# Turns of the attention cut by round instead of by forty units, VectorE's preparation in smaller steps, and rotated tiles turned in TensorE's transpose mode

## The reference

```python
B, S, _ = x.shape                                   # 4, 2048; H = 16 heads, D = 16, K = 4 nodes
node_probs = softmax(x @ Wr)                        # per token, head: 4 probabilities
expected_pos = cumsum(node_probs over tokens) - node_probs
pos = clip(expected_pos, 0.0, MAX_SEQ - 1)
cos, sin = table at floor(pos), linearly interpolated by frac(pos)
cos_w, sin_w = sum over nodes of node_probs * cos, node_probs * sin
q_r = q * cos_w + rotate_half(q) * sin_w            # k_r the same
node_w = einsum('bhik,bhjk->bhij', node_probs, node_probs)
scores = q_r k_r^T * SCALE + log(node_w + 1e-08)    # causal mask
out = softmax(scores) @ v, then @ Wo
```

## Time and profile before

| | |
|---|---|
| median of 3 runs | 2926.09 us (2920.56 to 2927.48) |
| the profiled execution's own time | 2932.58 us |
| its span, first to last instruction | 2930.5 us |
| mean granted TensorE clock over the span | 0.919 of full speed |
| attention, about | 430 to 2560 us of the span |

### The profile page before, as it was taken

How to read it: one execution, slowest core, us unless ns; L and a number is a source line. 1 busy time by engine, 2 the same in 40 slices (tenths; PEclk the granted TensorE clock), 3 DMA queues, 4 the chain that set the end, 5 groups by cost and what they waited for, 6 DMA issues and landing times. The chain is left out here.

```text
span 2930.5 us, 104065 instructions
## 1 busy us (share of the span) xinstructions
PE 2469.0 (84%) x45964; PEld 1911.6 (65%) x45964; DVE 1713.9 (58%) x3605; ACT 1674.0 (57%) x2102; POOL 990.7 (34%) x1423
## 2 busy tenths in 40 slices
PE   7278635587999999899999989999999999972786
PEld 4155412366688887778888777888778888741554
DVE  7733178888576567766566776656675111177331
ACT  6022133456677776667777767777766777560221
POOL 1078710243232224422222442322243222110787
PEclk9589966799999999999999999999999999985888
DMA  6455411121211112212111221111222111161555
GB/s 230 136 102 103 73 41 29 48 63 38 65 56 52 52 45 79 65 50 60 54 51 56 76 63 53 60 53 51 67 65 67 47 47 47 55 230 22 103 101 74
DMA packets 185106, 207.24 MB, mean 71 GB/s; under 512 B 35984, under 2 KB 151712, under 8 KB 184480
## 3 DMA queue, kind: packets, MB, share of 16 engines
q1 hardware_dynamic: 158880, 165.60, 18.6%
q0 software_dynamic: 24576, 34.10, 7.2%
q10 hardware_dynamic: 1152, 0.26, 0.0%
HBM read 131.68 MB, written 76.02 MB: 71 GB/s over the span
## 5 line engine op out<-in xcount | busy, mean ns | idle before, releaser
L1624 PEld LDWEIGHTS at_mix<-at_val,at_ew 128*64 128x64 f32 x34816 | 1227.6, 138 | 238.1 <-issue 35.4
L1208 ACT ACTIVATE at_ew<-at_ring 128x1024 f32<-128x1024 f32 (+1 forms) x1280 | 1125.3, 898 | 364.5 <-PE at_ring L1606 358.4
L1624 PE MATMUL at_mix<-at_val,at_ew 128*64 128x68 f32 x34816 | 1266.9, 224 | 41.1 <-DVE at_mixed L1470 28.1
L1606 PE MATMUL at_ring<-at_qT,at_kT 98*64 98x512 bf16 (+3 forms) x5120 | 699.7, 353 | 56.9 <-ACT at_ew L1208 36.0
L1129 POOL TENSOR_SCALAR_AFFINE_SELECT at_ew<-at_ew 128x256 f32<-128x256 f32 x512 | 294.4, 579 | 1077.8 <-ACT at_ew L1208 1076.9
L1470 DVE TENSOR_TENSOR at_mixed<-at_mix,at_prob 128x272 f32<-128x272 f32 x256 | 112.3, 439 | 440.0 <-PE at_mix L1624 438.6
L1606 PEld LDWEIGHTS at_ring<-at_qT,at_kT 98*64 98x64 bf16 x5120 | 228.7, 112 | 110.8 <-ACT at_ew L1208 48.2
L1151 POOL TENSOR_TENSOR at_val<-at_vo,at_val 128x256 f32<-128x256 f32 x384 | 266.7, 715 | 7.5
L315 POOL DMA_INDIRECT ffn_xn<-table,ffn_idx_all x128 | 123.8, 968 | 310.6 <-DMA ffn_idx_all<-ffn_idx_hi 272.2
L325 POOL DMA_INDIRECT out_dram<-ffn_xn,ffn_idx_all x128 | 210.3, 1643 | 52.6 <-issue 37.1
L1689 PE MATMUL at_side<-at_w_all,at_turned 128*64 128x512 f32 (+1 forms) x1024 | 203.5, 543 | 13.3 <-DVE at_bounded L1463 4.7
(11 more groups left out here) (224 smaller groups left out, 2769.9 us busy)
## 6 DMA issues: line engine op xcount, KB each, us to landing
table<-ffn_xn SPq DMA_DIRECT2D x32, 512.0 KB, 6.2
q_parts<-at_parts SPq DMA_DIRECT2D x64, 192.0 KB, 2.4
k_parts<-at_parts SPq DMA_DIRECT2D x64, 192.0 KB, 3.0
at_qT<-q_parts SPq DMA_DIRECT2D x128, 96.0 KB
at_kT<-k_parts SPq DMA_DIRECT2D x64, 192.0 KB
ffn_front<-in_L_attn_x_dram SPq DMA_DIRECT2D x16, 512.0 KB, 5.2
ffn_w_in<-in_L_ffn_w_dram SPq DMA_DIRECT2D x32, 256.0 KB, 3.8
at_xin<-out_dram SPq DMA_DIRECT2D x32, 256.0 KB, 5.8
```

What stands on the lines that cost most here:

```text
L1208: act.activation(ew[u % NE_BUF][:, a:b], ring[u % 2][:, a:b], ACT.Exp).then_inc(s["exp_ready"], 1)
L1606: lastm = pe.matmul(ring[u % 2][h:h + HALF, at:at + (CH - t) * P], kT[q][:, kc + j * P + h:kc + j * P + h + HALF], qT[q][:, qc + t * P:qc ...
L1624: m = pe.matmul(mix[block_of[u] % 2][h:h + HALF, t * K * VW:(t + 1) * K * VW], ew[u % NE_BUF][:, col + h:col + h + HALF], val[q][:, tile0 ...
```

## The change

1. Turns are cut by round. The first four stay at 24 units (SHORT, kind 0). Each second round gets 6 turns, of 37, 37, 38, 37, 37, 38 units (LONG, kind 1); each first round after the first gets 2 turns of 48 (WIDE, kind 2). There are 34 turns as before, and each turn has the same pairs new, fin and post.
2. A third table for WIDE on every engine, BURST = 28 there, and changed tables for the other two kinds.
3. VectorE's steps are cut: positions into positions, whole_positions and first_angles; angles into count_turns and angles; rotate into two halves and join_halves; in LONG and WIDE turns node_products and node_sums into four pieces each. No instruction is added or removed but that the pieces of 2048 elements become pieces of 1024 there.
4. turn_rotated on PE makes 8 full tiles in transpose mode instead of 16 matmuls of half a tile with the identity as moving operand.

```diff
-    SHORT, LONG = 24, 40
-    N_SHORT = 4
+    SHORT, LONG, WIDE = 0, 1, 2
+    SHORT_SIZE, N_SHORT = 24, 4
+    TURNS = {1: 6, 0: 2}
...
-    turns, at = [], 0
-    while at < U:
-        m = len(turns)
-        turns.append((at, SHORT if m < N_SHORT else LONG))
-        at += turns[-1][1]
+    rounds = [first_unit[v] for v in range(V) if v == 0 or visits[v][1] != visits[v - 1][1]] + [U]
+    turns = [(m * SHORT_SIZE, SHORT_SIZE, SHORT) for m in range(N_SHORT)]
+    assert rounds[1] == N_SHORT * SHORT_SIZE
+    for r in range(1, len(rounds) - 1):
+        size, count = rounds[r + 1] - rounds[r], TURNS[r % 2]
+        marks = [rounds[r] + size * n // count for n in range(count + 1)]
+        turns += [(a, b - a, LONG if r % 2 else WIDE) for a, b in zip(marks, marks[1:])]
...
-        return turns[m][0] + (18 if m < N_SHORT else 24) if m >= 0 else 0
+        return turns[m][0] + STORE_AT[turns[m][2]] if m >= 0 else 0
...
-        BURST = 26
+        BURST = (None, 26, 28)
...
-                    if at == (10 if short else 14) and new is not None:
+                    if at == (10, 14, 16)[kind] and new is not None:
                         add_up(new)
...
-                SHORT_AT = (3, 6, None, 8, 9, 12, 15, 18, 16, 23, 20)
-                LONG_AT = (4, 6, 10, 8, 16, 18, 20, 23, BURST + 2, BURST + 4, BURST + 3)
+                SHORT_AT = (3, 6, None, 8, 9, 12, 15, 19, 17, 23, 16)
+                LONG_AT = (4, 6, 10, 8, 16, 18, 20, 23, 28, 30, 25)
+                WIDE_AT = (3, 6, 10, 9, 19, 22, 25, 28, 30, 35, 27)
...
-                SHORT_AT = (0, 1, 6, 8, None, 10, 12, 13, 14, 18, 19, 20, 21, 23)
-                LONG_AT = (1, 2, 5, 8, 10, 14, 17, 20, 22, 30, 32, 25, 34, 33)
+                AT = {"weights": (1, 1, 1), "rotate": (2, 2, 10), "rotate_2": (2, 3, 13), "join": (3, 4, 14), "squares": (14, 20, 26),
+                      "bound": (20, 25, 31), "residual": (None, 10, 12), "shift": (6, 5, 6), "softmax": (8, 8, 9),
+                      "positions": (10, 14, 16), "whole": (10, 14, 17), "first_angles": (11, 15, 18), "count_turns": (12, 17, 20),
+                      "angles": (13, 18, 22), "statistics": (15, 22, 24), "normalise": (23, 36, 46)}
+                PRODUCTS_AT = ({18: 0, 21: 2}, {30: 0, 32: 1, 33: 2, 34: 3}, {34: 0, 37: 1, 40: 2, 43: 3})
+                SUMS_AT = ({19: 0, 22: 2}, {31: 0, 33: 1, 34: 2, 35: 3}, {36: 0, 39: 1, 42: 2, 45: 3})
...
                             for n in range(4):
                                 for g in range(G):
-                                    for h in range(0, P, HALF):
-                                        at = (g * 4 + n) * P + h
-                                        lastm = pe.matmul(side[h:h + HALF, n * GP + g * P:n * GP + (g + 1) * P],
-                                                          qkr[:, at:at + HALF], ident[:, :],
-                                                          start=(n % 2 == 0 and g == 0), stop=False, skip_group_check=True)
+                                    at = (g * 4 + n) * P
+                                    lastm = pe.matmul(side[:, n * GP + g * P:n * GP + (g + 1) * P], qkr[:, at:at + P], ident[:, :],
+                                                      is_transpose=True, start=(n % 2 == 0 and g == 0), stop=False, skip_group_check=True)
...
                 SHORT_AT = (1, 4, None, None, 9, 10, 13, 16, 19, 21)
-                LONG_AT = (1, 3, 7, 9, 13, 15, 17, 20, 24, BURST)
+                LONG_AT = (1, 3, 7, 9, 13, 15, 17, 20, 24, 26)
+                WIDE_AT = (1, 4, 8, 11, 15, 20, 23, 26, 30, 33)
```

More of the change, by code:

```diff
@@ L987, in schedule @@
             first_visit()
-            for m, (start, size) in enumerate(turns):
-                for at in range(min(size, U - start)):
-                    unit(start + at, at, size == SHORT, new_of(m), fin_of(m), posts.get(m))
+            for m, (start, size, kind) in enumerate(turns):
+                for at in range(size):
+                    unit(start + at, at, kind, new_of(m), fin_of(m), posts.get(m))
             last_projections()
@@ L1059, in first_visit, with unit @@
                     load_heads(1)
-                def unit(u, at, short, new, fin, post):
+                def unit(u, at, kind, new, fin, post):
                     if u + 2 in first_unit and u + 2 < U:
@@ L1546, in unit @@
                         mix_nodes(u - 2)
-                    where = SHORT_AT if short else LONG_AT
-                    step = where.index(at) if at in where else None
                     more = new is not None and new + 1 < TP
-                    if step == 0 and fin is not None:
-                        turn_weights()
-                    if step == 1 and fin is not None:
-                        rotate(fin)
-                    if step == 2 and new is not None:
-                        shift_logits(new)
@@ L1556, in unit @@
-                    if step == 3 and new is not None:
-                        node_softmax(new)
-                    if step == 4 and post is not None:
-                        add_residual(post, 0, 1)
-                    if step == 5 and new is not None:
-                        positions(new)
-                    if step == 6 and new is not None:
-                        angles(new)
-                    if step == 7 and fin is not None:
-                        largest_squares(fin)
-                    if step == 8 and more:
-                        statistics(new + 1)
@@ L1568, in unit @@
-                    if step == 9 and new is not None:
-                        node_products(new)
-                    if step == 10 and new is not None:
-                        node_sums(0)
-                    if step == 11 and fin is not None:
-                        bound(fin)
-                    if step == 12 and new is not None:
-                        node_sums(2)
-                    if step == 13 and more:
-                        normalise(new + 1)
+                    step = [name for name in AT if AT[name][kind] == at]
@@ new lines, in unit @@
+                    per = 2 if kind == SHORT else 1
+                    if fin is not None:
+                        if "weights" in step:
+                            turn_weights()
+                        if "rotate" in step:
+                            rotate(fin, 0)
+                        if "rotate_2" in step:
+                            rotate(fin, 1)
+                        if "join" in step:
+                            join_halves()
+                        if "squares" in step:
+                            largest_squares(fin)
+                        if "bound" in step:
+                            bound(fin)
@@ L1579, in last_projections @@
+                    if more:
+                        if "statistics" in step:
+                            statistics(new + 1)
+                        if "normalise" in step:
+                            normalise(new + 1)
                 def last_projections():
```

84 lines of the change are left out of this document (59 added, 25 removed).

## The result

The changed kernel takes **2960.03 us** (median of 4 runs, 2952.87 to 2965.93); the kernel before, run beside it, 2926.78 us (4 runs, 2920.56 to 2929.29). The ratio is 1.0116, with a 95% interval of 1.0088 to 1.0143: 34 us slower. The forecast was 17 us slower, 2943 us, with a range of 2897 to 2960. The profiled execution took 2965.93 us, its span is 2963.8, its granted clock 0.914 (0.919 before).

What follows compares the result with a forecast made beforehand. PE was taken to set the time in rounds 1, 3, 5 and 7, and to idle mostly for VectorE's foldings in 2, 4 and 6. Terms -13 - 25 + 19 + 22 + 14 = +17 us gave 2943 us, range 2897 to 2960.

Steps and rivals of the forecast that it cites:

- Item 1: turn_rotated on PE: full tiles in transpose mode save 0.54 us per pair in 24 turns, -13 us.
- Item 2: Rounds 2, 4 and 6: PE's 28.0 us of waits for VectorE's foldings nearly go with small steps, -25 us.
- Item 3: Four short turns: next_rsqrt ahead of trig makes VectorE wait for ScalarE, 4.8 us per turn, +19 us.
- Item 4: Five wide turns: PE waits 3.1 us for ScalarE's trig, next_rsqrt about 1.3 us more, +22 us.
- Item 5: Ends of long turns, rounds 1, 3, 5: PE's turn_inputs waits for normalise, 2.7 us per three turns, +14 us.
- rival D: VectorE bounds wide turns: foldings lag, items 3 and 5 reach upper bounds, PE's clock drops; +33, 2959 us, chance 0.13.

Runs made afterwards that it cites:

- run 5: Kernel before with turns cut by round and rotated tiles in transpose mode, every table of steps as before: 2880.55 us, ratio 0.9848 to the kernel before.
- run 7: 6 with, in wide turns, trig at unit 35, copy_qk at 37, next_rsqrt at 29, products and sums from 37 and 38: ratio 0.9878 to the kernel before.
- 6: Changed kernel with the edits of run 2 and run 3 together: ratio 0.9916 to the kernel before, 59 us less than the changed kernel.
- run 1: Kernel before with turn_rotated's tiles in transpose mode and nothing else: ratio 0.9936 to the kernel before, -19 us.
- run 4: Kernel before with its turns cut by round, all tables of steps as before: ratio 0.9907 to the kernel before, -27 us.
- run 2: Changed kernel with ScalarE's short-turn table as before (next_rsqrt 20, trig 16, low_part 18): ratio 1.0061 to the kernel before, 16 us less than the changed kernel.
- 10: Changed kernel with only the wide-turn edit of run 7: ratio 1.0057 to the kernel before, 17 us less than the changed kernel.
- run 3: Changed kernel with normalise at unit 29 of long and 33 of wide turns, not 36 and 46: ratio 0.9966 to the kernel before, 44 us less than changed.
- run 9: Changed kernel with normalise at unit 29 in long turns, still 46 in wide: ratio 1.0006 to the kernel before, 32 us less than the changed kernel.

## Why the prediction was wrong

The sign was right and the size was half. With the runs, the path from the kernel before is: turns and tiles -44, VectorE's steps and their places +9 (5 to 7), the wide turns' trig +11 (7 to 6), both tables +59 (6 to the changed kernel): **+34 us**, the measured time.

- **Item 1, tiles, forecast -13: -19** (run 1). A pair gives 1.74 - 1.03 - 0.10 = 0.61 us, where I had 0.54: the four more tiles take 0.11 each, not 0.13. That is 15 us in 24 turns; another 2 are in round 0 of run 1 (202.0 us beside 203.9), which I had at 0 to 4 together with the lead.
- **Item 2, foldings, forecast -25: -27** (run 4). The size is right by luck. The turns alone gave the gain, with no small step in the kernel, and the foldings' waits fell there from 28.0 us only to 17.3; the rest of the gain is other waits and a higher clock. The profile of the changed kernel shows 1.7, 1.7 and 0.6 us of such waits left, as forecast, but there PE stood for ScalarE instead: with trig moved they are 8.0 us in round 2 again (run 7).
- **Item 3, next_rsqrt in short turns, forecast +19: +16** (run 2). All its marks are there: ScalarE idle 5.92, VectorE 4.50 where 4.6 was forecast, round 0 longer by 17.9.
- **Item 4, trig in wide turns, forecast +22: +11 to +17** (runs 7 and 10). The wait is 3.15 us where 3.1 was forecast, in four of the five wide turns, and 2.02 in the other. The price came out below the sum of waits, since in its absence foldings wait.
- **Item 5, normalise at the turns' ends, forecast +14: +44** (run 3), of which the long turns are 32 and the wide ones 12 (run 9). **This is the step that failed.** It took waits of "1.7, 0.6 and 0.4" for three positions of a turn, in rounds 1, 3 and 5. PE waits there in all 18 long turns, for 1.75, 1.28 and 1.37 us in the three positions, and for 2.35 instead of 1.37 in the last of each round: 29.3 us in all. The first position is as forecast. The second is longer because normalise's first two operations take 0.87 us more there, beside POOL's work; the third because VectorE stands idle for 0.88 us (up to 1.83 in the last of a round) ahead of normalise, where the check for the next heads is. These take up 15 of the 29.3 us, a sum over the rows of the 18 ends, and what is left is the 14 forecast. That account is read from the trace and was not put to a run. And the sum had no term at all for normalise at unit 46 of 48: waits of 2.33 and 2.14 us at the end of the first wide turn of a round, of 1.54 and 1.37 at that of the second, worth 12 us with what follows them (run 9).
- **The clock** was in rival D alone, and there as something that follows from VectorE's lag. It is part of what the waits for xn cost: 10 us of PE's busy time in rounds 2 and 4 (135.7 + 136.6 beside 130.3 + 131.9 with normalise early).
- **No term for VectorE's new steps and their places.** They cost 9 us (5 to 7), 3.5 of them in round 0, where VectorE's chain is the time and where no instruction was cut, and a little in the long turns. The cut itself is cheap: 92 more instructions, and VectorE busy for 1728.8 us in 7 beside 1727.8 in 5. The 15 us by which it is busier than before the change stand in 5 already, which has only whole steps.
- Rival D named the place from which it would decide ("a step stands for more than about 2 us ahead of a folding") and 2959 us. The time is near, the mechanism isn't: foldings didn't lag, xn did. (A third of the way from +17 to +62 is +32, not +33.)

## What to carry to other kernels

A step moved to the end of a turn can cost a wait in every turn, whatever the engine's busy share: lay out what stands ahead of it in each position and each kind of turn, branches and checks that leave no row included, and price every kind. Read the granted clock behind each wait of 2 us and more, and add what it costs. A change that bundles layout and step tables should be taken apart before it is judged: here turns and tiles were worth 44 us, and the tables and steps written with them took away 78. Cutting a step into pieces helps only where the pieces fall into time that is free; a long step that filled an idle stretch whole may be the better one, and on a queue that runs in order a step that reads a late result stops every step behind it.

## What the runs showed of the chip

- In the changed kernel the granted clock fell to about 0.5 behind all five waits of 2.14 to 2.35 us for xn, for some 3 to 6 us: at once and for 6 us behind the 2.35 us that end at 1127.5, but only some 3 us after PE had gone on behind the 2.34 us that end at 1643.5 (0.89 in the first 3 us, 0.54 in the next). Behind waits of 1.28 to 1.75 us it stayed at 1.00. Behind the waits of 2.04 and 2.26 us for foldings in run 5's round 2 it stayed at 1.00 too, for all of the next 9 us, and behind one of 2.02 us for ScalarE in the changed kernel. So length alone doesn't say whether it falls.
- Small operations of VectorE with two operands, 0.16 us elsewhere, took 0.62 and 0.57 us while POOL worked on at_val (887.90 to 889.16), and did so again in every long turn at that position.
- Float32 tiles of 128x128 in transpose mode have records of 0.27 us each, but eight in a row take 1.09 us, 0.12 us from one to the next. The Trainium skill, TensorE: Matmul & The Clock Gate, Part 4, gives about 0.28 us for one bf16 tile in a kernel; the float32 record is as long, and the row shows that it is no price for a group. It also says that transposes don't raise the clock; with 2.4 us of them (this step, turn_inputs and turn_outputs) in turns of some 58, no run here can show it.
